# The order of a DMA queue's list: the rows of the maximum ahead of the stores of the bfloat16 parts

## The chip, the cores and the metric

One core of one Trainium2 chip runs the whole kernel as one launch. The metric is the device time of that core in microseconds (us).

## The reference

The input x is 32 x 256 x 128 (batch, sequence, model width), float32. Two attentions with 16 heads of width 8 are added to it and the sum is normalized; then a top-1 mixture of 8 experts with a capacity of 1024 tokens each follows, and a second layer norm.

```python
xl = _layer_norm(x, ln_l_g, ln_l_b)          # for the local attention
xg = _layer_norm(x, ln_g_g, ln_g_b)          # for the global one
for i in range(0, B, 40):                    # B = 32: one window, over the batch axis
    o = _mha(xl[:50, i:end], ...)            # sequence positions 0..31 only (axis 1 cut at B)
for i in range(0, B, 50):                    # one chunk: full attention in each sequence
    glb = glb.at[i:i+50].set(_mha(xg[i:i+50], ...))
x = _layernorm(x + local + glb)
x = _layernorm(x + moe(x))                   # route, W1, relu, W2, weighted by the gate
```

In the attention, s = q k^T, a = softmax(s), and the output is a v, projected. The local part touches positions 0 to 31 of each sequence, the global part all 256.

## The kernel before, in words

**Units and pairs.** The attention runs over 36 units: u = 0 to 3 are the local ones (8 sequences of 32 positions each), u = 4 to 35 the global ones (one sequence of 256 positions each). Inputs are normalized and projected in pairs of units, p = u // 2, 18 pairs in all. The program is a software pipeline written by hand: for each engine there is a function `step(u)` or `fill(u, hp, e)`, called for u = 0 to 39, and in step u the engines hold pieces of several units. "Step u" below is the stretch in which TensorE computes the exponent's scores of unit u and, between them, the scores of unit u + 1 from which the maximum of each row is taken.

**Scores in six bfloat16 parts.** Queries and keys are float32 and are split into three bfloat16 parts (`part`), made by ScalarE, VectorE and GpSimd. SP stores them, in six DMAs of 128 to 384 KB, into `q_stack` and `k_stack` in DRAM (`store_stacks`, L328), six terms a head. It then loads them back in another layout (`load_stack`, L357; `qs` and `ks` hold two units, each in two halves of four head pairs), 48 partitions of terms for each head. The loads for pair p wait for the semaphore of the landing of all six stores of p. The stores of pair u // 2 + 1 stand in the even step u, and the loads of its first half for unit u + 2 stand later in the same step.

**The rows of the maximum.** For unit u + 1 TensorE computes the scores once in `ps_a` (L512), VectorE takes the maximum of each row (`take_max`, L926), GpSimd splits it into three bfloat16 parts (`split_max`, L1153 to L1157), TensorE turns it (`turn_max`, L571), and ScalarE copies it to `mT` (`copy_max`, L766). SP puts it into three more partitions of `qs` (`place_max`, L383, two DMAs of 6 KB). The second computation of the scores (`exp_pass`, L535, into `ps_b`) has the maximum subtracted by these rows, and ScalarE takes the exponential (L759). All this is done in halves of a unit: half 0 has head pairs 0 to 3, half 1 the pairs 4 to 7. TensorE waits for the rows of half 0 at the start of step u and for those of half 1 in its middle:

```python
if e == 1 and hp % 4 == 0:
    pe.wait_ge(max_rows[hp // 4], 32 * (u + 1))
```

`place_max(u, 1)` waits for `mT_ready` at 2u + 2, which ScalarE sets early in step u, after its first exponential. `place_max(u + 1, 0)` is the last thing of SP's step u in most steps.

**What sets the order on SP.** SP only issues DMAs and waits; its list is the order of the code of its `step(u)`, and an instruction that waits holds all behind it. In a step with all its parts the list has: loads of unit u + 1 half 1; the six stores (even steps 2 to 32); rows of the maximum of unit u half 1; the residual (`load_xr`, L366 or L375 to L377); an output (`store_o1`, L403, or in the local units `store_y`, L389); the input of a later pair (`load_x`, L318, even steps up to 26); loads of unit u + 2 half 0; rows of unit u + 1 half 0. In steps 3 to 6 it also clears a part of `routed` (`clear_routed`, L397, two DMAs of 520 KB), and at the end of step 7 it issues the weights of two experts (L1319 to L1322). SP's DMAs all go to one hardware queue, q1.

**Other users.** GpSimd adds the bias to the residual when it has landed (`bias_residual`, L1167), and after that, in even steps, normalizes the inputs of a later pair (L1129, L1135); its next `split_max` stands behind. After the attention, 16 chunks of 512 tokens go through the experts (L1332 to L1479).

Of the kernel before, what the change touches and what calls it, by code (L numbers as in the profile page):

```python
# [44 lines left out]
def wait(eng, sem, value):  # L45

    if value > 0:
        eng.wait_ge(sem, value)
# [28 lines left out]
def is_local(u):  # L77
    return u < LU


def there(u):
    return 0 <= u < U


def routes(u):
    return LU <= u < U
# [30 lines left out]
def layer(nc, ctx, c, x, needed_first, needed_later, blockq_in, blockk_in, q_stack, k_stack, x_local, routed, out,  # L117
# [175 lines left out]
    def first_pair(s):  # L293

        return s // 2 + AHEAD if s % 2 == 0 and s // 2 + AHEAD < NPAIR else None
# [12 lines left out]
    def _(sp):  # L308
        def load_x(p):

            b = p % 3
            wait(sp, xh_ready, p - 2)
            if kind(p):
                for t in range(4):
                    n = 4 * (4 * p + t)
                    sp.dma_start(xt[:, b, t], x[n:n + 4, 0:LW, :]).then_inc(x_loaded[b], 16)
            else:
                sp.dma_start(xt[:, b], rows(x_t, 4 * (p - LPAIR), 4).rearrange("t p d -> p t d")).then_inc(x_loaded[b], 16)  # L318

        def store_stacks(p):  # L320
            sp.wait_ge(part2_ready, p + 1)
            for s, stack in enumerate((q_stack, k_stack)):
                for k, (t0, n) in enumerate(((0, 3), (3, 2), (5, 1))):
                    if s == 0:
                        src = part[:, p % 2, 0, k:k + 1, :].to_broadcast([P, n, PAIR])
                    else:
                        src = part[:, p % 2, 1, 0:n, :]
                    sp.dma_start(stack[p, :, t0:t0 + n, :], src).then_inc(stack_stored[p % 2], 16)  # L328
# [11 lines left out]
        def load_stack(u, half):  # L340

            h, p = u % 2, u // 2
            wait(sp, scores, 8 * (u - 2) + 4 * half + 4)
            sp.wait_ge(stack_stored[p % 2], 96 * (p // 2 + 1))
            if u < 2:
                sp.wait_ge(stacks_cleared, 2)
            if u in (LU, LU + 1):

                for e in range(2):
                    at = HALF * e + MASKROW  # L350
                    sp.dma_start(qs[at:at + NBLK, h, 4 * half:4 * half + 4, :],
                                 nomask[:]).then_inc(stack_loaded[h][half], 16)
            for dst, stack in ((qs, q_stack), (ks, k_stack)):
                src = stack[p, 64 * half:64 * half + 64, :, h * S:(h + 1) * S]
                src = src.rearrange("(g e d) t n -> e (d t) g n", e=2, d=DH)
                for e in range(2):
                    sp.dma_start(dst[HALF * e:HALF * e + STACK, h, 4 * half:4 * half + 4, :],  # L357
                                 src[e]).then_inc(stack_loaded[h][half], 16)

        def load_xr(u):  # L360
            h = u % 2

            wait(sp, y_ready, u - 1)
            if is_local(u):
                for t in range(2):
                    sp.dma_start(xr[:, h, t], x[8 * u + 4 * t:8 * u + 4 * t + 4, 0:LW, :]).then_inc(xr_loaded[h], 16)  # L366
                return

            if u == LU:
                sp.wait_ge(y_stored[0], 32)  # L370
            if u == LU + 3:
                sp.wait_ge(y_stored[0], 64)
                sp.wait_ge(y_stored[1], 64)
            at = batch(u)
            sp.dma_start(xr[0:LW, h, 0], x_local[at]).then_inc(xr_loaded[h], 16)  # L375
            sp.dma_start(xr[LW:P, h, 0], x[at, LW:P, :]).then_inc(xr_loaded[h], 16)
            sp.dma_start(xr[:, h, 1], x[at, P:S, :]).then_inc(xr_loaded[h], 16)  # L377

        def place_max(u, half):
            sp.wait_ge(mT_ready, 2 * u + half + 1)  # L380
            for e in range(2):
                at = HALF * e + MAXROW
                sp.dma_start(qs[at:at + 3, u % 2, 4 * half:4 * half + 4, :],  # L383
                             mT[12 * e:12 * e + 12, half, :]).then_inc(max_rows[half], 16)

        def store_y(u):
            sp.wait_ge(y_ready, u + 1)
            for t in range(2):
                sp.dma_start(x_local[8 * u + 4 * t:8 * u + 4 * t + 4],  # L389
                             y[:, u % 2, t]).then_inc(y_stored[u % 2], 16)  # L390

        def clear_routed(u):

            sp.wait_ge(constants_set, 1)
            for k in range(2):
                first = (2 * (u - LU + 1) + k) * (T // 8)
                sp.dma_start(routed[first:first + T // 8].rearrange("(t p) r -> p t r", p=P),  # L397
                             c["empty"][:].unsqueeze(1).to_broadcast([P, T // P // 8, ROW])).then_inc(routed_cleared, 16)

        def store_o1(u):  # L400
            g = batch(u)
            sp.wait_ge(o1_ready, g + 1)
            sp.dma_start(rows(out, g, 1).rearrange("o (t p) d -> p (o t) d", p=P), o1[:]).then_inc(o1_stored, 16)  # L403

        def step(u):
            p = first_pair(u)
            if there(u + 1):
                load_stack(u + 1, 1)
            if u % 2 == 0 and u >= 2 and u // 2 + 1 < NPAIR:
                store_stacks(u // 2 + 1)  # L410
            if there(u):
                place_max(u, 1)
                load_xr(u)
            if routes(u - 3):
                store_o1(u - 3)
            if there(u - 2) and is_local(u - 2):
                store_y(u - 2)
            if p is not None and p + 2 < NPAIR:
                load_x(p + 2)
            if there(u + 2):  # L420
                load_stack(u + 2, 0)
            if there(u + 1):
                place_max(u + 1, 0)
            if LU - 1 <= u < LU + 3:
                clear_routed(u)
            if u == LU + 3:
                tail.first_weights(sp)
# [11 lines left out]
        for u in range(U + 4):  # L439
            step(u)  # L440
# [1111 lines left out]
```

## Time and profile before

| | |
|---|---|
| median of 3 runs | 808.11 us (806.39 to 810.08) |
| the profiled execution's own time | 806.47 us |
| its span (first to last instruction) | 804.4 us |
| TensorE matmul / weight load busy | 698.3 us (87%) / 352.4 us (44%) |
| VectorE / ScalarE / GpSimd busy | 571.7 (71%) / 489.6 (61%) / 498.5 us (62%) |
| DMA queue q1 | 139824 packets, 85.35 MB, 37.0% of 16 engines' span |
| mean granted TensorE clock | 0.917 of full speed |

The attention takes the first 634 us of the span, the experts the rest. Busy shares are means over the span. PE is the matmul engine, PEld its weight loads, DVE VectorE, ACT ScalarE, POOL GpSimd; SPq is SP's queue of DMA issues. A name like "qs<-mT" says that mT is copied into qs. The profiled execution lies 1.64 us under the median of the runs.

### The profile page before, as it was taken

What the parts mean: (1) busy time and instruction counts of PE and PEld (TensorE: products, weight loads), DVE (VectorE), ACT (ScalarE), POOL (GpSimd) and SP (SyncE); (2) the same over time, 40 slices, a digit from 0 to 9 for tenths busy, and PEclk for the clock granted to TensorE, in tenths of its full rate; (3) what the DMA queues carried; (4) which work ended last, traced back from release to release, by engine and by line L of the source; (5) the groups of instructions that cost most, each with busy time, mean ns of one, the idle gap of its engine ahead of it and who ended that gap; (6) DMA issues with size and microseconds to landing.
All of it is one profiled execution on the core that took longest, in us unless ns stands there. A gap on an engine that the chain in (4) does not pass through costs nothing.

```text
span 804.4 us, 19344 instructions
## 1 busy us (share of the span) xinstructions
PE 698.3 (87%) x6502; PEld 352.4 (44%) x6502; DVE 571.7 (71%) x1703; ACT 489.6 (61%) x882; POOL 498.5 (62%) x1015
## 2 busy tenths in 40 slices
PE   1579779798999999999999999899999828999991
PEld 1434333343444444444444444344434415777771
DVE  5455577676988889889898898877888211666664
ACT  1335456575878677778787777777777614344340
POOL 4432323546677776777777878775765660667666
PEclk9755798888999999999999999999999958999996
DMA  3532576846254343552543534424431111343321
GB/s 89 174 127 60 158 188 141 207 108 211 63 175 145 107 154 86 156 166 83 173 142 111 155 109 138 154 75 146 128 114 51 32 29 51 103 128 95 98 76 35
DMA packets 145778, 95.36 MB, mean 119 GB/s; under 512 B 14404, under 2 KB 137885, under 8 KB 145680
## 3 DMA queue, kind: packets, MB, share of 16 engines
q1 hardware_dynamic: 139824, 85.35, 37.0%
q0 software_dynamic: 4096, 7.81, 3.0%
q10 hardware_dynamic: 1760, 0.96, 0.5%
q8 instruction: 53, 0.87, 0.5%
q14 instruction: 45, 0.37, 0.2%
HBM read 47.70 MB, written 45.74 MB: 116 GB/s over the span
## 4 chain that ended last, share of the span: by engine, by line
PE 62%; SPq 17%; DMA 7%; POOL 5%; issue 4%; DVE 3%; ACT 2%; POOLq 0%; ACTq 0%; DVEq 0%
PE ps_b L535 15%; PE ps_o L561 15%; SPq L328 8%; PE ps_a L1365 6%; DMA qs<-mT 5%; PE ps_b L1359 5%; SPq L357 5%; PE ps_f L476 3%; PE ps_f L481 3%; PE ps_f L471 2%; SPq L383 2%; POOL out L1479 2%; PE ps_a L512 2%; PE ps_f L1359 1%; PE ps_m L571 1%
## 5 line engine op out<-in xcount | busy, mean ns | idle before, releaser
L926 DVE TENSOR_REDUCE mx<-ps_a 128x2 f32<-128x512 f32 (+1 forms) x576 | 374.1, 656 | 119.0 <-PE ps_a L512 111.8
L759 ACT ACTIVATE prob<-ps_b 128x1024 f32<-128x1024 f32 (+1 forms) x288 | 281.1, 976 | 110.1 <-PE ps_b L535 97.0
L535 PE MATMUL ps_b<-qs,ks 59*128 59x256 bf16 (+1 forms) x1152 | 224.1, 277 | 32.1 <-DMA qs<-mT 29.6
L512 PE MATMUL ps_a<-ks,qs 56*128 56x256 bf16 (+1 forms) x1152 | 223.8, 279 | 7.2 <-DVE mx L926 4.8
L561 PE MATMUL ps_o<-prob,vp 128*32 128x256 f32 (+1 forms) x2304 | 184.8, 395 | 0.0
L535 PEld LDWEIGHTS ps_b<-qs,ks 59*128 59x128 bf16 x1152 | 67.0, 95 | 193.7 <-issue 113.5
L1153 POOL CAST mpart<-mx 128x16 bf16<-128x16 f32 x72 | 14.2, 197 | 123.5 <-DVE mx L926 123.2
L1217 POOL DMA_INDIRECT routed<-row,slot x64 | 67.3, 1051 | 31.5 <-issue 26.3
L1479 POOL DMA_INDIRECT out<-res,dest x64 | 64.8, 1013 | 34.2 <-DVE res L1454 19.1
L561 PEld LDWEIGHTS ps_o<-prob,vp 128*32 128x32 f32 x2304 | 46.8, 111 | 61.8 <-issue 54.9
L512 PEld LDWEIGHTS ps_a<-ks,qs 56*128 56x128 bf16 x1152 | 65.2, 96 | 12.9 <-DVE mx L926 8.7
L1404 ACT ACTIVATE prob<-ps_b,b_sb 128x512 f32<-128x512 f32 x48 | 33.0, 687 | 59.6 <-PE ps_b L1359 58.0
L766 ACT COPY mT<-ps_m 24x256 bf16<-24x256 bf16 x72 | 26.1, 362 | 59.7 <-PE ps_m L571 59.4
L1365 PE MATMUL ps_a<-w_sb,prob 128*128 128x128 f32 x512 | 59.6, 275 | 0.0
L1365 PEld LDWEIGHTS ps_a<-w_sb,prob 128*128 128x128 f32 x512 | 58.4, 192 | 0.5 <-issue 0.5
L1135 POOL TENSOR_SCALAR xh<-xt,fmv,frstd 128x128 f32<-128x128 f32 x72 | 57.1, 806 | 1.9
L1190 POOL TENSOR_SCALAR row<-y,mv,rstd 128x128 f32<-128x128 f32 x64 | 51.0, 799 | 0.0
L1142 POOL TENSOR_TENSOR part<-rest,part 128x512 bf16<-128x512 f32 x36 | 41.0, 1159 | 10.2 <-ACT part L734 10.2
L1359 PE MATMUL ps_b<-xT,w_sb 128*128 128x512 f32 x96 | 45.6, 613 | 0.0
L1435 DVE SCALAR_TENSOR_TENSOR z<-ps_a,rows_sb,xb 128x128 f32<-128x128 f32 x64 | 18.1, 344 | 32.8 <-PE ps_a L1365 32.8
L1167 POOL TENSOR_TENSOR xr<-xr,bo_sb 128x256 f32<-128x256 f32 x36 | 26.1, 726 | 21.4 <-DMA xr<-x 21.0
L1179 POOL TENSOR_TENSOR rstd<-veps,powm 128x4 f32<-128x4 f32 x32 | 33.3, 1040 | 2.7
(122 smaller groups left out, 1043.2 us busy)
## 6 DMA issues: line engine op xcount, KB each, us to landing
qs<-q_stack SPq DMA_DIRECT2D x144, 96.0 KB
ks<-k_stack SPq DMA_DIRECT2D x144, 96.0 KB
q_stack<-part SPq DMA_DIRECT2D x18, 384.0 KB
k_stack<-part SPq DMA_DIRECT2D x18, 384.0 KB
q_stack<-part SPq DMA_DIRECT2D x18, 256.0 KB
k_stack<-part SPq DMA_DIRECT2D x18, 256.0 KB
routed<-empty SPq DMA_DIRECT2D x8, 520.0 KB, 6.4
rows_sb<-routed SPq DMA_DIRECT2D x16, 260.0 KB, 3.8
```

What stands on the lines that cost most here:

```text
L328: sp.dma_start(stack[p, :, t0:t0 + n, :], src).then_inc(stack_stored[p % 2], 16)
L512: ins = nc.tensor.matmul(ps_a[:, e, qt * S:qt * S + keys.stop - keys.start], qs[half, h, hp, qt * P:(qt + 1) * P], ks[half, h, hp, keys], ...
L535: ins = nc.tensor.matmul(ps_b[:, exp_bank(hp, e), kt * n:(kt + 1) * n], ks[half, u % 2, hp, kt * P:(kt + 1) * P], qs[half, u % 2, hp, quer ...
L561: last = nc.tensor.matmul(ps_o[32 * j:32 * j + 32, col:col + n], vp[:, u % 6, kt, 4 * q + j, :], prob[:, hp, at:at + n], start=(q % 2 == 0 ...
L759: nc.scalar.activation(prob[:, hp, 0:2 * n].rearrange("p (a n) -> p a n", a=2), src, ACT.Exp).then_inc(exp_done, 1)
L926: nc.vector.reduce_max(mx[:, u % 2, :, col], ps_a[:, e].rearrange("p (t k) -> p t k", t=2)[:, :, 0:k], axis=AX).then_inc(max_done, 1)
L1135: last = nc.gpsimd.tensor_scalar(xh[:, p % 2, t], xt[:, p % 3, t], fmv[:, p % 2, t, 0:1], frstd[:, t:t + 1], ALU.subtract, ALU.mult)
L1190: last = nc.gpsimd.tensor_scalar(row[:, g % 3, t, 0:D], y[:, u % 2, t], mv[:, t, 0:1], rstd[:, 0, t:t + 1], ALU.subtract, ALU.mult)
L1217: pool.indirect_dma_start(out=routed, out_offset=bass.IndirectOffsetOnAxis(ap=slot[:, g % 3, t:t + 1], axis=0), in_=row[:, g % 3, t, :], i ...
L1359: nc.tensor.matmul(ps_h[f], w1_sb[:, he, f * P:(f + 1) * P], xT[:, hk], start=True, stop=True).then_inc(hidden, 1)
L1365: last = nc.tensor.matmul(ps_y[:, bank, t * D:(t + 1) * D], hT[:, hk, f, t * P:(t + 1) * P], w2_sb[:, he, f], start=(f == 0), stop=(f == F ...
L1479: pool.indirect_dma_start(out=out_rows, out_offset=bass.IndirectOffsetOnAxis(ap=dest[:, h, t:t + 1], axis=0), in_=res[:, h, t], in_offset= ...
```

## The change

In SP's `step(u)`, `place_max(u, 1)` is called before `store_stacks(u // 2 + 1)` and no longer behind it. Nothing else is changed.

```diff
             p = first_pair(u)
             if there(u + 1):
                 load_stack(u + 1, 1)
+            if there(u):
+                place_max(u, 1)
             if u % 2 == 0 and u >= 2 and u // 2 + 1 < NPAIR:
                 store_stacks(u // 2 + 1)
             if there(u):
-                place_max(u, 1)
                 load_xr(u)
```

How it moves SP's instructions in one of the global even steps, before (the semaphores that an instruction waits for stand in brackets; from the loads of unit u + 1 to the first-half rows of unit u + 1):

```order
L357 DMA qs<-q_stack 48x4x256 [waits stack_stored1,scores]
L357 DMA qs<-q_stack 48x4x256
L357 DMA ks<-k_stack 48x4x256 x2
L328 DMA q_stack<-part 128x3x512 [waits part2_ready]
...
L328 DMA k_stack<-part 128x512
L383 DMA qs<-mT 3x4x256 [waits mT_ready]
L383 DMA qs<-mT 3x4x256
L375 DMA xr<-x_local 32x128 [waits y_ready]
...
L318 DMA xt<-x 128x4x128 [waits xh_ready]
L357 DMA qs<-q_stack 48x4x256 [waits stack_stored0,scores]
...
L383 DMA qs<-mT 3x4x256 [waits mT_ready]
```

And the same step in the changed kernel:

```order
L357 DMA qs<-q_stack 48x4x256 [waits stack_stored1,scores]
L357 DMA qs<-q_stack 48x4x256
L357 DMA ks<-k_stack 48x4x256 x2
L383 DMA qs<-mT 3x4x256 [waits mT_ready]
L383 DMA qs<-mT 3x4x256
L328 DMA q_stack<-part 128x3x512 [waits part2_ready]
...
L328 DMA k_stack<-part 128x512
L375 DMA xr<-x_local 32x128 [waits y_ready]
...
L318 DMA xt<-x 128x4x128 [waits xh_ready]
L357 DMA qs<-q_stack 48x4x256 [waits stack_stored0,scores]
...
L383 DMA qs<-mT 3x4x256 [waits mT_ready]
```

The first pair of rows, with its wait for mT, stands ahead of the six stores; the residual, the input, the loads of the next unit and the first-half rows keep their order behind the stores.

The first even step that has stores is step 2, a local one. There SP's list differs in the same way:

```order
-L328 DMA q_stack<-part 128x3x512
-L328 DMA q_stack<-part 128x2x512
-L328 DMA q_stack<-part 128x512
-L328 DMA k_stack<-part 128x1536
-L328 DMA k_stack<-part 128x1024
-L328 DMA k_stack<-part 128x512
-L383 DMA qs<-mT 3x4x256 x2
+L383 DMA qs<-mT 3x4x256 x2
+L328 DMA q_stack<-part 128x3x512
+L328 DMA q_stack<-part 128x2x512
```

The two issues of the rows pass the six stores. In each of the 16 even steps from 2 to 32 this happens once; in the other steps there is nothing between which the order could change.

## Rows read from the trace of the kernel before

**Rows 1.** The page's chain of work that ended last, by line, shares of the span.
```profile
PE ps_b L535 15%; PE ps_o L561 15%; SPq L328 8%; PE ps_a L1365 6%; DMA qs<-mT 5%; PE ps_b L1359 5%; SPq L357 5%; PE ps_f L476 3%; PE ps_f L481 3%; PE ps_f L471 2%; SPq L383 2%; POOL out L1479 2%; PE ps_a L512 2%; PE ps_f L1359 1%; PE ps_m L571 1%
```

**Rows 2.** Table of waits, whole span: us in total, times, longest us.
```profile
PE ps_b L535 <- DMA qs<-mT: 29.6, 19, 5.6
```

**Rows 3.** Table of waits of TensorE, stretch 205 to 512 us (steps 9 to 27).
```profile
PE ps_b L535 <- DMA qs<-mT: 6.8, 9, 1.9
```

**Rows 4.** Table of waits of TensorE, stretch 512 to 604 us (steps 28 to 33).
```profile
PE ps_b L535 <- DMA qs<-mT: 3.6, 3, 1.9
```

**Rows 5.** Timeline of SP, step 10: start us, us, engine, line, operation, out<-in, count.
```profile
222.07 1.69 SPq L328 DMA_DIRECT2D q_stack<-part  x3
223.81 2.41 SPq L328 DMA_DIRECT2D k_stack<-part  x3
226.26 1.64 SPq L383 DMA_DIRECT2D qs<-mT  x2
227.95 0.43 SPq L375 DMA_DIRECT2D xr<-x_local  x1
...
230.40 2.24 SPq L357 DMA_DIRECT2D qs<-q_stack  x2
232.68 0.93 SPq L357 DMA_DIRECT2D ks<-k_stack  x2
233.65 1.49 SPq L383 DMA_DIRECT2D qs<-mT  x2
236.25 0.80 SPq L357 DMA_DIRECT2D qs<-q_stack  x2
```

**Rows 6.** Timeline, ScalarE and TensorE, steps 10 and 11; idle time before and releaser in brackets.
```profile
224.32 0.36 ACT L766 COPY mT<-ps_m 24x256 bf16<-24x256 bf16 x1 [0.45 <-PE ps_m L571]
...
229.14 0.28 PE L535 MATMUL ps_b<-qs,ks 59*128 59x256 bf16 x1 [0.52 <-DMA qs<-mT]
...
237.51 0.28 PE L535 MATMUL ps_b<-qs,ks 59*128 59x256 bf16 x1
...
240.25 0.28 PE L571 MATMUL ps_m<-ident_bf,mpart 128*24 128x128 bf16 x2
```

**Rows 7.** Timeline of TensorE: start of step 3, middles of steps 4, 6, 8, 12.
```profile
95.70 0.23 PE L535 MATMUL ps_b<-qs,ks 59*128 59x128 bf16 x1 [0.37 <-DMA qs<-mT]
...
121.62 0.39 PE L535 MATMUL ps_b<-qs,ks 59*128 59x256 bf16 x1 [5.59 <-DMA qs<-mT]
...
156.53 0.39 PE L535 MATMUL ps_b<-qs,ks 59*128 59x256 bf16 x1 [3.63 <-DMA qs<-mT]
...
195.22 0.39 PE L535 MATMUL ps_b<-qs,ks 59*128 59x256 bf16 x1 [3.35 <-DMA qs<-mT]
...
261.50 0.28 PE L535 MATMUL ps_b<-qs,ks 59*128 59x256 bf16 x1 [1.08 <-DMA qs<-mT]
```

**Rows 8.** Stretches: length, each engine's busy us (instructions), granted clock, DMA share, GB/s.
```profile
156.50:169.00 12.50, 12.25 (x84) 4.70 (x86) 6.33 (x10) 6.02 (x10) 5.11 (x8) 0.61 0.60 136
195.20:205.70 10.50, 10.26 (x82) 4.12 (x82) 6.72 (x15) 5.81 (x10) 4.89 (x7) 0.76 0.33 93
229.10:237.50 8.40, 8.13 (x82) 3.78 (x82) 6.62 (x15) 6.02 (x12) 6.69 (x16) 1.00 0.42 116
261.50:271.30 9.80, 9.57 (x82) 3.90 (x83) 6.71 (x15) 5.82 (x10) 6.33 (x14) 0.83 0.35 99
520.30:530.20 9.90, 9.65 (x84) 4.09 (x86) 6.71 (x15) 5.85 (x10) 5.71 (x11) 0.83 0.26 73
...
223.00:228.00 5.00, 4.99 (x59) 2.05 (x51) 4.65 (x15) 4.47 (x9) 4.32 (x8) 1.00 1.02 347
...
112.00:117.00 5.00, 3.28 (x42) 1.39 (x38) 3.89 (x7) 4.28 (x6) 0.73 (x4) 1.00 1.17 199
```

**Rows 9.** Timeline of GpSimd, steps 10 and 11.
```profile
231.44 0.72 POOL L1167 TENSOR_TENSOR xr<-xr,bo_sb 128x256 f32<-128x256 f32 x1
...
237.46 0.20 POOL L1153 CAST mpart<-mx 128x16 bf16<-128x16 f32 x1 [1.07 <-DVE mx L926]
```

## The prediction

> **What bounds the kernel now.** First the page's chain of work that ended last: its matmul lines lead, and the queue of SP stands in it with the stores (L328), the loads (L357) and the rows of the maximum (L383), beside "DMA qs<-mT" with 5% [rows 1]. Then the table of waits: TensorE waited 19 times for the rows of the maximum, 29.6 us in all [rows 2]. Sixteen of these stand in the sixteen even steps with stores (steps 2 to 32): nine of 6.8 us in steps 10 to 26 [rows 3], three of 3.6 us in steps 28 to 32 [rows 4], and, after 3.2 us for three waits elsewhere (0.37 of them at the start of step 3 [rows 7], the others before step 1), 16.0 us in steps 2, 4, 6 and 8, where single waits are 5.59, 3.63 and 3.35 us [rows 7].
>
> Step 10 shows the mechanism. SP issues six stores from 222.07 to 226.22, and the rows of the second half only then, at 226.26 [rows 5], although ScalarE had written mT by 224.68 [rows 6]. TensorE starts at 229.14 after 0.52 us of waiting [rows 6]. So it was ready at 228.62, 3.94 us after mT, and the rows took 2.88 us from their issue. From 229.14 to the start of step 11 at 237.51 TensorE needs 8.37 us [rows 6]: without the wait a step would end 3.94 + 8.37 = 12.3 us after mT.
>
> **The change, part by part.**
>
> *The wait that goes.* Issued at 224.70, the rows land at about 227.6, 1.0 us before TensorE is ready. The same holds wherever the queue is free, so all waits of the even steps but step 4's go.
>
> *The wait that comes.* SP now stands still before the stores until mT is there: in step 10 from 222.07 to 224.70, 2.6 us. Everything behind moves by that: six stores, three parts of the residual, the output, the input of a later pair, the loads for step 12 and the first-half rows of step 11. The last are due at the start of step 11, and now landed about 233.65 + 2.85 = 236.5, only 1.0 us early [rows 5]. Counted from the end of mT the new order is: rows 1.5, stores 4.15 (222.07 to 226.22), what lies from 227.95 to 230.40, 2.45, loads 1.8 to 3.25, first-half rows to landing 2.85. The loads take 3.25 where their first two issues need 2.24 as in step 10, 1.8 where they need 0.80 as at 236.25 [rows 5]. That gives 12.7 to 14.2 us, if SP's issuing is the limit. The loads also wait for the stores' landing. The stores' bytes flow at 347 GB/s from 223 to 228, with the DMA engines full [rows 8]; the loads were issued 8.33 us after the first store, so the landing took at most that. If it takes all of it, the chain is 1.5 + 8.33 + 1.8 + 2.85 = 14.5. I take the middle between 12.7 and 14.5, 13.6, since step 10 shows neither end alone. TensorE would be there at 12.3, so it waits x = 1.3 us at the start of each odd step, with bounds 0.4 and 2.2.
>
> The Trainium skill, DMA: Bandwidth & Descriptors (Anatomy of one DMA), says that the fixed cost of about 2 us lies mostly in the write receipt and is longest for HBM. By it the stores would land 1 + 5 + 2 us after their issue, an estimate from that page's figure, and the chain would be 14.2. The trace has the loads 2.4 us after the last full slice, which does not exclude it.
>
> *Sum by steps, with x for the new wait.* (Each of the first five stretches of rows 8 runs from the middle of an even step to the start of the next.)
> - Steps 10 to 26 without 12, eight of them: 8x minus their waits of 6.8 - 1.1 = 5.7.
> - Step 12: wait 1.08, then 9.8 us to the next start instead of 8.4, at a granted clock of 0.83 [rows 7, 8]: x - 2.5.
> - Steps 28 to 32: waits 3.6, and step 28 has 9.9 us after its wait at a clock of 0.83 [rows 8], 1.5 more than 8.4. No input is left to load, which shortens the chain by 0.5 each. Step 32, whose matmuls are fewer (no projections are due there), gets some 0.9 less: 3x - 1.5 - 3.6 - 1.5 + 0.9 = 3x - 5.7.
> - Step 6: wait 3.63, then 12.5 us at a clock of 0.61 [rows 7, 8]; without the idle time before it I take 8.4: x - 7.7.
> - Step 8: wait 3.35, then 10.5 us at 0.76 [rows 7, 8]; its stores are issued among weight loads, for which I add 0.4: x - 5.1.
> - Step 4: the rows no longer wait for the stores, but still for loads behind the clearing of routed, with the DMA engines full from 112 to 117 [rows 8]. TensorE was ready at 121.62 - 5.59 = 116.0 and the rows would land near 117.6, so its wait could fall by 4.0. But the stores fill the same DMA engines and land hardly earlier, and the loads wait for them. Between 0 and 4.0 I take 2.5, nearer to the upper end since step 5's start has some slack over its rows.
> - Step 2: step 3 already starts on a wait for its own rows, 0.37 us [rows 7], so the 3.4 us saved in step 2 are waited there again: 0.
>
> Together 14x - 29.2. With x = 1.3 that is -11.0. The half clock follows idle time: after the waits of 1.08 (step 12) and 1.95 (step 28) the clock fell [rows 4, 7, 8], while after step 10's it stayed at 1.00 [rows 8]. New waits of 1.3 can do the same; I allow two such dips at 1.4 us, +2.8. **Sum: -8.2 us.** The profiled execution took 806.47, which becomes 798.3; the median of the runs shown is 808.11, 1.6 us higher, and becomes 799.9, say 800.0.
>
> *Edits at nothing.* The number of issues, bytes and matmuls is unchanged. The residual's load comes 2.6 us later. In step 10 GpSimd starts on it at 231.44 and idles 1.07 us before the first split of step 11 [rows 9]. Loaded by some 9.5 us after mT instead, it pushes GpSimd's 5 us of work behind it, and the split ends near 15.7 after mT; TensorE wants it 2.74 us into step 11 (240.25), at 16.3 with x = 1.3. So the new wait covers it. Without that cover (x = 0) it would hold TensorE 0.6 us a step. The second-half rows of odd steps wait for mT and absorb up to 1.5 us of backlog on SP.
>
> **Rivals.**
> 1. *Slower: the first-half rows land late.* Place: SP's queue in even steps, from the landing of the stores to the start of the odd step. If stores land late and the loads are issued slowly as well, 1.5 + 8.33 + 3.25 + 2.85 = 15.9, x is up to 3.6. The sum passes zero at x = 2.1 (1.9 with two dips), and with x = 2.6 and five dips it is 36.4 - 29.2 + 7.0 = +14.2, or 822. For it: the stores at 347 GB/s leave nothing free, and rows 5 show loads taking 3.25. Against it: the two slow parts exclude each other, because the queue drains while SP waits for a landing. The rule named above gives a chain of 14.2 and x = 1.9, no change: it is part of the next case.
> 2. *No change.* x between 1.6 and 2.1, or x = 1.3 with dips after most new waits, 14 times 1.4 = +20 against -11. Time 804 to 812. The trace has dips after two waits of over 1 us and none after others of the nine, so dips after all are unlikely. The Trainium skill, TensorE: Matmul & The Clock Gate (Part 1), says that the throttled state is the default and activity releases it; by it each new idle stretch risks the half clock, as in step 12.
> 3. *Full gain.* The stores land early and the first-half rows are on time: x near 0, -29 us, plus 0.6 a step for GpSimd, about 784. For it: the stores no longer share with the loads before them. Against it: even SP's bare issuing gives 12.7.
> 4. *The change does not do what it says:* the rows ahead of the stores land no sooner. Then nothing is saved and 2.6 us a step come on top. Odd steps speak against it: there rows meet no stores and TensorE does not wait.
>
> **How the numbers follow.** About 0.5% (4 us) is what a measurement can tell from no change. My forecast, the rows' wait moved and shortened, with x from 0.4 to 1.6: 0.57; full gain 0.05; together faster by over 0.5%: 0.62. No change: 0.20. Slower, rival 1 with rival 4: 0.18. At the bounds, x = 0.4 without dips gives -23.6 (784) and x = 2.2 with five dips +8.6 (817); the range leaves out a tenth on each side: 789 to 811. The forecast's own range is 785 to 804.
>
> **What would show it.** In the table of waits "PE ps_b <- DMA qs<-mT" should be about 20 us instead of 29.6, in some 13 waits at the starts of odd steps, each 0.4 to 2.2, and none at the second half of an even step but step 4's. SP should wait for ScalarE's mT at every even step, about 2.6 us more in each of the regular steps. The clock after steps 6 and 8 should be near 1.0. It is wrong if the new waits exceed 2 us on average, if half-clock stretches follow most of them, or if TensorE waits for GpSimd's mpart in odd steps.

## The result, and the profile after

The change made the kernel slower, not faster: 813.59 us median of 20 runs (804.56 to 823.73) against 806.62 (20 runs of the kernel before beside them), a ratio of 1.008 with a 95% interval of 1.0046 to 1.0113. A second set on another chip gave 1.0128 (1.0088 to 1.0168). The forecast was 800.0, with a range to 811. The profiled execution of after took 820.7 us (span 818.6) against 806.47 (span 804.4), 14.2 us more. Ratios are taken over the runs within 1.5% of the fastest of their kernel and medians over all runs, so a ratio is not always the quotient of two medians, and this profiled execution of after is one of the slower runs left out of its ratio. So the 14.2 us of the two profiles are about twice what the change costs by the ratio (6.5 us), and what follows from them is checked below against a second profile of the same kernel.

The page of after: the row of busy times, and the granted clock in 40 slices (before in the second fence).

```profile
PE 717.3 (88%) x6502; PEld 357.0 (44%) x6502; DVE 578.1 (71%) x1703; ACT 491.1 (60%) x882; POOL 497.6 (61%) x1015
PEclk9855658999999999999897999999999957999996
```
```profile
PEclk9755798888999999999999999999999958999996
```

TensorE is busy 717.3 us instead of 698.3 with the same instructions, which is more than the whole difference of the two spans: the loss is slower matmuls and not idle time. Slices 5 and 6 fell from 7 and 9 to 6 and 5, slices 8 to 10 rose from 8 to 9, and an 8 and a 7 stand at 20 and 22, in the middle of the attention, where before had nines. The table of waits of after, whole span:

```profile
PE ps_b L536 <- DMA qs<-mT: 24.3, 18, 3.9
```

Against [rows 2] that is 24.3 us for 29.6. No wait at the middle of an even step is left, and sixteen stand at the starts of the odd steps 3 to 33: 3.86 us at step 3, then 0.92, 0.80, 0.76, 1.56, 0.50, 2.34, 1.75, 0.53, 1.42, 1.82, 0.52, 1.55, 0.96, 0.44 and 1.81; that is 21.5 us in all, and 17.7 without step 3, 1.18 each for the fifteen of steps 5 to 33. The other two are before step 1.

The queue of SP and the two waits of step 10 in after, which answer to [rows 5] and [rows 6]. First SP:

```profile
221.38 1.47 SPq L383 DMA_DIRECT2D qs<-mT  x2
222.90 1.61 SPq L328 DMA_DIRECT2D q_stack<-part  x3
224.55 2.06 SPq L328 DMA_DIRECT2D k_stack<-part  x3
226.65 1.01 SPq L375 DMA_DIRECT2D xr<-x_local  x1
...
229.82 0.47 SPq L318 DMA_DIRECT2D xt<-x  x1
230.59 0.82 SPq L357 DMA_DIRECT2D qs<-q_stack  x2
231.46 0.93 SPq L357 DMA_DIRECT2D ks<-k_stack  x2
232.43 1.49 SPq L383 DMA_DIRECT2D qs<-mT  x2
```

Then ScalarE's copy and TensorE at the start of step 11, and three of the later odd starts:

```profile
221.00 0.36 ACT L767 COPY mT<-ps_m 24x256 bf16<-24x256 bf16 x1 [0.45 <-PE ps_m L572]
...
235.15 0.39 PE L536 MATMUL ps_b<-qs,ks 59*128 59x256 bf16 x1 [1.56 <-DMA qs<-mT]
...
369.93 0.28 PE L536 MATMUL ps_b<-qs,ks 59*128 59x256 bf16 x1 [0.53 <-DMA qs<-mT]
...
402.87 0.39 PE L536 MATMUL ps_b<-qs,ks 59*128 59x256 bf16 x1 [1.42 <-DMA qs<-mT]
...
509.06 0.28 PE L536 MATMUL ps_b<-qs,ks 59*128 59x256 bf16 x1 [1.55 <-DMA qs<-mT]
```

mT is written at 221.36. The rows go out in 1.5 us, the first store at 222.90, the loads at 230.59, 7.69 us later, the first-half rows at 232.43, and TensorE starts 2.72 us after that: 1.5 + 7.7 + 1.8 + 2.7 = 13.8 us after mT. It was ready at 235.15 - 1.56 = 233.59, 12.2 after mT.

Where the time went is read from the stretches of after: steps 0 to 4, steps 5 to 9, steps 10 to 33, and then what follows five of the new waits (steps 11, 15, 19, 21, 23):

```profile
47.20:137.00 89.80, 82.69 (x716) 36.96 (x716) 50.51 (x114) 42.56 (x76) 27.04 (x59) 0.58 0.40 116
137.00:218.20 81.20, 77.18 (x798) 33.75 (x799) 68.28 (x173) 61.41 (x108) 49.41 (x115) 0.98 0.65 169
218.20:622.10 403.90, 382.52 (x3869) 167.93 (x3868) 333.23 (x895) 298.99 (x546) 283.13 (x649) 0.95 0.41 126
235.20:244.10 8.90, 8.90 (x80) 3.39 (x82) 7.02 (x19) 5.23 (x9) 7.14 (x15) 0.82 0.22 62
302.20:311.20 9.00, 9.00 (x80) 3.54 (x82) 6.95 (x19) 5.23 (x9) 6.57 (x14) 0.81 0.27 79
369.90:377.50 7.60, 7.57 (x78) 3.26 (x78) 6.78 (x19) 5.18 (x9) 6.11 (x14) 1.00 0.34 92
402.90:414.50 11.60, 11.60 (x78) 3.93 (x78) 7.27 (x19) 5.38 (x9) 7.21 (x15) 0.59 0.23 69
440.00:451.80 11.80, 11.77 (x78) 3.96 (x78) 7.20 (x19) 5.49 (x9) 6.93 (x14) 0.57 0.21 61
```

The same three stretches of steps in the kernel before:

```profile
47.20:130.70 83.50, 70.56 (x717) 32.54 (x717) 49.02 (x114) 41.33 (x76) 28.03 (x60) 0.72 0.47 129
130.70:221.50 90.80, 81.89 (x799) 34.78 (x798) 68.78 (x174) 61.99 (x109) 48.93 (x113) 0.91 0.58 147
221.50:607.60 386.10, 369.19 (x3871) 165.51 (x3872) 328.10 (x895) 298.18 (x546) 284.30 (x649) 0.99 0.43 132
```

Three pieces, then (length, and the granted clock in the third column from the right): +6.3 us in steps 0 to 4 (at 0.58 of the clock instead of 0.72), -9.6 in steps 5 to 9 (0.98 instead of 0.91), +17.8 in steps 10 to 33 (0.95 instead of 0.99); the rest of the span gives the missing -0.3.

For the last piece the table of waits of TensorE over steps 10 to 33, of after and then of before:

```profile
PE ps_b L536 <- DMA qs<-mT: 15.2, 12, 2.3
```
```profile
PE ps_b L535 <- DMA qs<-mT: 10.4, 12, 1.9
```

Twelve waits each, 4.8 us more after. The other 13 us are the clock. The first half of an odd step takes 7.6 us at the full clock (the stretch from 369.9, after a wait of 0.53). It takes 8.9 or 9.0 where a half-clock stretch of 3.4 us falls in it (a stretch at 0.50 of full speed, as from 235.0 to 238.4), and 11.6 or 11.8 where one of 10.2 us does (granted 0.59 and 0.57). In steps 10 to 33 seven of the twelve new waits are followed by one: five of the short kind, at 1.1 to 1.5 us each, and two of the long kind, at 4.0 and 4.2, together 15.1 us, where before had two at 1.4 and 1.5. The difference, 12.2, and the waits' 4.8 make 17.0 of the 17.8.

### The profile page after: what moved, and what is told of

Same layout as the page of the kernel before. It is cut to its first block, busy times and chain, and to the rows that moved or that the text cites. A ratio compares the mean times of both kernels' runs of the same rounds, so it can differ in the third digit from the quotient of the medians.

```text
span 818.6 us, 19344 instructions
## 1 busy us (share of the span) xinstructions
PE 717.3 (88%) x6502; PEld 357.0 (44%) x6502; DVE 578.1 (71%) x1703; ACT 491.1 (60%) x882; POOL 497.6 (61%) x1015
## 4 chain that ended last, share of the span: by engine, by line
PE 64%; SPq 12%; DMA 9%; issue 5%; POOL 5%; ACT 3%; DVE 2%; POOLq 0%; ACTq 0%; DVEq 0%
PE ps_b L536 16%; PE ps_o L562 15%; PE ps_a L1366 6%; PE ps_b L1360 5%; SPq L357 4%; DMA qs<-mT 4%; SPq L383 3%; SPq L328 3%; PE ps_f L482 3%; DMA k_stack<-part 3%; PE ps_f L472 3%; PE ps_m L580 2%; PE ps_a L513 2%; PE ps_m L572 2%; POOL out L1480 2%
## 5 line engine op out<-in xcount | busy, mean ns | idle before, releaser
L536 PE MATMUL ps_b<-qs,ks 59*128 59x256 bf16 (+1 forms) x1152 | 229.8, 284 | 26.3 <-DMA qs<-mT 24.3
L513 PE MATMUL ps_a<-ks,qs 56*128 56x256 bf16 (+1 forms) x1152 | 230.6, 287 | 9.4 <-DMA ks<-k_stack 4.9
L562 PE MATMUL ps_o<-prob,vp 128*32 128x256 f32 (+1 forms) x2304 | 191.4, 409 | 0.0
```

Source lines behind the costliest of these rows:

```text
L513: ins = nc.tensor.matmul(ps_a[:, e, qt * S:qt * S + keys.stop - keys.start], qs[half, h, hp, qt * P:(qt + 1) * P], ks[half, h, hp, keys], ...
L536: ins = nc.tensor.matmul(ps_b[:, exp_bank(hp, e), kt * n:(kt + 1) * n], ks[half, u % 2, hp, kt * P:(kt + 1) * P], qs[half, u % 2, hp, quer ...
L562: last = nc.tensor.matmul(ps_o[32 * j:32 * j + 32, col:col + n], vp[:, u % 6, kt, 4 * q + j, :], prob[:, hp, at:at + n], start=(q % 2 == 0 ...
```

## The experiments

Ratios are to runs of the kernel before on the same chip, 95% intervals in brackets; kernels of one chip stand together. On the first of these chips (its before: 812.75 us) ran four.

**The change again.** No edit to the changed kernel.

> The changed kernel again, for a second profile. Theory C (the new waits at the start of odd steps are of the size forecast, and the half clock that follows them costs more than the waits that went): time 1.005 to 1.012 of before; waits for qs<-mT 20 to 26 us in all, all at starts of odd steps, and 5 to 9 stretches of half clock between 200 and 610 us, each starting just after one of these waits. Rival W (the waits themselves grew, the clock is chance): the waits for qs<-mT add up to more than 33 us, and half-clock stretches in that part are 0 to 2 as before. Rival S (chance at the start: the half clock in steps 1 to 4 lasts longer for reasons that have nothing to do with the change): the excess lies before 130 us.

Measured: 820.63 us, 1.0128 (1.0088 to 1.0168), just above what was expected. The change costs something on either chip. Steps 10 to 33 took 404.4 us, as in the first profile:

```profile
215.40:619.80 404.40, 380.14 (x3871) 167.26 (x3872) 333.16 (x895) 298.75 (x546) 285.29 (x649) 0.97 0.41 126
```

The waits are not the same. Those for the rows were 7.2 us, 6 times, in these steps (19.0 us in the whole span, against the 20 to 26 expected), beside thirteen waits of 0.4 to 0.9 us for prob, of which more below. Six half-clock stretches lie in these steps. Four begin at a wait for the rows; one begins 2.4 us after a wait for prob (0.80 us), and one begins at 269.9, on a wait of 0.47 us for the loads of ks. So "each starting just after one of these waits" did not hold.

**The new order in steps 2 to 8 only**, and **in steps 10 to 32 only.** The edit for the first; the second has `ahead = u >= 10`.

```
+ahead = u < 10
-if there(u):
+if there(u) and ahead:
     place_max(u, 1)
 if u % 2 == 0 and u >= 2 and u // 2 + 1 < NPAIR:
     store_stacks(u // 2 + 1)
 if there(u):
+    if not ahead:
+        place_max(u, 1)
```

> The new order in steps 2 to 8 only, the old one in steps 10 to 32. Before, the waits in steps 4, 6 and 8 took 12.6 us and were followed by half clock; after, the starts of steps 5, 7 and 9 wait 0.8 to 0.9 each. Theory C: 8 to 14 us faster than before (0.983 to 0.990). Rival S (the early part is where the change loses): slower than before by 3 us or more.

> The new order in steps 10 to 32 only. Before, these twelve steps waited 10.4 us in their middles; in the changed kernel the starts of the odd steps behind them waited 15.2 us. Theory C: plus 5 us of waits and 8 to 15 us of half clock, so 12 to 20 us slower than before (1.015 to 1.025), with 5 or more half-clock stretches in 235 to 610 us. Rival W: 3 to 7 us slower (1.004 to 1.009), with no more half clock than before. With e1_early it should add up to the whole change within 4 us.

Measured: early 808.42, 0.9887 (0.9841 to 0.9933), though 0.995 by the medians of all runs; late 826.4, 1.017 (1.011 to 1.023), and by the medians the same. The product of the ratios, 1.0055, is 5.9 us short of the whole, 1.0128 on this chip: more than the 4 us expected, but within the intervals. One edit is two: a gain of 0.5 to 1.1% in the early steps and a loss of 1.7% in the regular ones. Steps 10 to 33 of the two kernels, early and then late:

```profile
219.20:610.30 391.10, 371.34 (x3869) 165.92 (x3868) 329.30 (x895) 298.39 (x546) 285.06 (x649) 1.00 0.43 130
```
```profile
218.70:625.70 407.00, 382.35 (x3871) 167.80 (x3872) 332.88 (x895) 298.67 (x546) 285.29 (x648) 0.96 0.41 125
```

The loss is 15.9 us, at 0.96 of the clock for 1.00, and TensorE's busy time has 11.0 of it. Nine half-clock stretches lie in these steps of late and one in those of early. Six of the nine begin at or within 1.3 us of one of the six waits for rows (1.04 to 1.69 us), three 2.4 to 2.6 us after a wait of 0.8 us for prob.

Over all profiles, the half-clock stretches in steps 10 to 33 count as follows. Order of before: 2, 1, 1 and 1 (before, the kernel before once more, early, and the order in steps 4 to 8 only). New order: 7, 6, 9 and 4 (after, again, late, and with other work out of the chain). Split: 1, 0 and 0. That the new order brings them does not rest on one profile.

**The six stores split**: those of q_stack ahead of the rows, those of k_stack behind them, in all even steps.

```
-def store_stacks(p):
+def store_stacks(p, which=(0, 1)):
     for s, stack in enumerate((q_stack, k_stack)):
+        if s not in which:
+            continue
...
+if stores:
+    store_stacks(u // 2 + 1, (0,))
 if there(u):
     place_max(u, 1)
+if stores:
+    store_stacks(u // 2 + 1, (1,))
```

> The three stores of the queries, then the rows of the maximum, then the three stores of the keys. SP would idle 2.6 us before mT is there; now it issues three stores in that time, and the rows have only three stores ahead of them. The rows should land about 2.7 us after mT as in the changed kernel, and the stores about when they land in the kernel before. Theory C, with the chain as I count it: no waits of over 0.3 us in regular steps, neither in the middle nor at the start, waits for qs<-mT under 8 us in all, no half clock between 200 and 600 us, time 770 to 788 us (0.955 to 0.977). Rival F (rows behind any stores are late, since all share one queue and its engines): waits of 0.3 to 1 us stay in the middles of even steps, time within 1% of before.

Measured: 804.02, 0.9871 (0.9809 to 0.9932). The gain is there, smaller than expected. In steps 10 to 33 TensorE waits for no rows at all:

```profile
216.20:603.40 387.20, 369.93 (x3871) 165.24 (x3872) 330.12 (x895) 297.36 (x546) 285.04 (x649) 1.00 0.43 131
```

But it waits elsewhere, in even steps, for ScalarE's prob (whole span):

```profile
PE ps_b L541 <- ACT prob L765: 8.4, 21, 0.8
```

On the next chip (before: 807.91) ran two.

**The change, with TensorE kept at work in the new waits**: twelve more matmuls (128x128 bf16, identity on identity, into a bank that is overwritten) ahead of the wait at the start of each odd step from 3 to 33. The output is not altered.

```
 if kt == 0:
+    if e == 1 and hp == 0 and u % 2 == 1 and 3 <= u <= 33:
+        wait(pe, exp_done, 8 * u + hp - e)
+        for _ in range(12):
+            nc.tensor.matmul(ps_b[:, exp_bank(hp, e), 0:P], c["ident_bf"][:],
+                             c["ident_bf"][:], start=True, stop=True)
```

> The changed kernel with twelve extra bf16 matmuls of 128x128 (on the identity, into the bank that the next scores overwrite) in TensorE's program at the start of each odd step from 3 to 33, ahead of the wait for the rows: 16 times about 0.7 to 1.2 us of work put where TensorE idles 0.5 to 2.3 us. The output doesn't depend on it. Theory C: the idle stretches shrink below 1 us, nearly all half-clock stretches between 200 and 610 us vanish, and the kernel with more work is 4 to 12 us faster than the changed one, so 0.993 to 1.003 of before. Rival W (the clock's stretches don't follow from these waits): as slow as the changed kernel or up to 8 us slower (1.008 to 1.018), with as many half-clock stretches.

Measured: 804.53, 0.9991 (0.994 to 1.0042). More work takes less time: the 0.8 to 1.3% that the change costs are gone. Steps 10 to 33:

```profile
218.00:609.50 391.50, 377.22 (x4015) 173.77 (x4014) 332.03 (x895) 298.13 (x546) 283.20 (x649) 0.99 0.43 130
```
```profile
PE ps_b L541 <- DMA qs<-mT: 7.3, 9, 1.3
```

That is 144 matmuls more and 12.4 us less than in the first profile of after, which is of another chip; the same steps in the order of before differ by up to 5.0 us from chip to chip (386.1, 391.1, 390.4). Half clock followed two of these starts instead of seven. TensorE's busy time is 377.2 instead of 382.5 although it does more. The change itself was not run on this chip.

**SP waits for mT, and the stores stay ahead**: the standstill of the change without its earlier rows.

```
 if u % 2 == 0 and u >= 2 and u // 2 + 1 < NPAIR:
+    sp.wait_ge(mT_ready, 2 * u + 2)
     store_stacks(u // 2 + 1)
 if there(u):
     place_max(u, 1)
```

> SP waits for mT ahead of the six stores, as in the changed kernel, but the rows stay behind the stores, as before: the changed kernel's stall without its gain. The rows of the even steps then land 4.15 + 2.85 us or more after mT, where TensorE is ready 3.9 us after it: a wait of about 3 us in the middle of each of the twelve later even steps. Both theories: 30 to 60 us slower than before (1.04 to 1.075); theory C has half clock after nearly every such wait, so the upper half of that range, Rival W has it in fewer than four, so the lower half.

Measured: 860.78, 1.072 (1.0616 to 1.0824). Steps 10 to 33:

```profile
219.80:661.60 441.80, 400.52 (x3869) 171.45 (x3868) 328.68 (x895) 298.65 (x546) 283.71 (x649) 0.90 0.38 115
```
```profile
PE ps_b L536 <- DMA qs<-mT: 34.9, 12, 3.8
```

The waits rise by 34.9 - 10.4 = 24.5 us against the first profile of the kernel before (another chip), TensorE's busy time by 400.5 - 369.2 = 31.3, with the same matmuls. Each of the twelve waits (2.73 to 3.76 us) is followed by a half-clock stretch, of 3.4 to 10.2 us. A standing queue costs more through the clock than by the wait itself.

The third chip (before: 810.21) had four.

**The kernel before, once**, for a profile on this chip.

> The kernel before once more, for a second profile from this series. All theories: time 0.99 to 1.01 of before; waits for qs<-mT of 20 to 30 us, at the middles of even steps; step 3 at full clock; the half-clock stretches from 130 to 610 us number 3 to 6 and follow the longer of these waits.

Measured: 815.8 us in its one run. Its steps 0 to 4 took 87.2 us at a clock of 0.54, where the first profile of the same kernel, on another chip, took 83.5 at 0.72. So nearly 4 us in steps 0 to 4 lie within what two profiles of one kernel differ by. And its steps 10 to 33 hardly wait for rows, against what was expected:

```profile
PE ps_b L535 <- ACT prob L759: 8.1, 14, 1.0
...
PE ps_b L535 <- DMA qs<-mT: 2.4, 4, 0.9
```
```profile
228.32 0.36 ACT L766 COPY mT<-ps_m 24x256 bf16<-24x256 bf16 x1 [0.92 <-PE ps_m L571]
```

ScalarE's copy of mT comes 0.92 us after its idle time began where it was 0.45 [rows 6], and TensorE waits 0.8 us for prob in even steps. On such a chip TensorE is itself late, the old middle wait is mostly covered, and less is left to win in the regular steps. All eight profiles of this chip and of that of the first four runs have such waits for prob in steps 10 to 33, and none of the six of the other chips has.

**The new order in steps 4, 6 and 8 only** (`ahead = 4 <= u < 10`).

> The new order in steps 4, 6 and 8 only. In the four profiles with the new order in step 2 the half clock lasted without a break from about 95 to 130 us (steps 3 and 4), with a wait of 1.4 to 6.9 us at the start of step 3; with the old order in step 2 it did not. Theory C: leaving step 2 as it was saves those 30 us at half clock, so this is 4 to 12 us faster than the new order in steps 2 to 8, 0.970 to 0.985 of before. Rival S (the half clock there is chance or belongs to the loss of step 4's waits): the same as e1_early, 0.984 to 0.993, and half clock from 95 to 130 us again.

Measured: 803.09, 0.9899 (0.9843 to 0.9954), against 0.9887 with step 2, on another chip: step 2 is worth nothing, as predicted, and what it costs is within the intervals of about 0.5%. Its profile has no half clock in step 3, but it has 9.9 us of it in step 5. The low clock of that part moves about and does not come from one edit.

**The change, with other work out of the chain**: in steps 10 to 32 the output, the input and the residual are issued ahead of the rows, while SP waits for mT anyway.

```
+early = u % 2 == 0 and 10 <= u <= 32
+if early:
+    if routes(u - 3):
+        store_o1(u - 3)
+    if p is not None and p + 2 < NPAIR:
+        load_x(p + 2)
+    load_xr(u)
 if there(u):
     place_max(u, 1)
...
-if there(u):
+if there(u) and not early:
     load_xr(u)
-if routes(u - 3):
+if routes(u - 3) and not early:
     store_o1(u - 3)
...
-if p is not None and p + 2 < NPAIR:
+if p is not None and p + 2 < NPAIR and not early:
     load_x(p + 2)
```

> The changed kernel, with the output, the input and the residual of the even steps 10 to 32 issued in the time in which SP would wait for mT: ahead of the rows and not behind the stores. That takes 2.45 us of issues out of the chain from mT to the first-half rows. If SP's issues set that chain (rival I), the waits at the starts of odd steps from 11 on fall to 0 to 0.3 us, and the time to 0.975 to 0.99 of before. If the landing of the stores sets it (theory L; in the changed kernel the loads were issued within 0.1 us of the landing in nine of twelve steps), the waits fall by at most 0.5 us each and the time stays 0.995 to 1.01 of before.

Measured: 819.92, 1.01 (1.006 to 1.0141), no better than the change. SP in its step 10:

```profile
217.48 1.50 SPq L383 DMA_DIRECT2D qs<-mT  x2
219.02 1.62 SPq L328 DMA_DIRECT2D q_stack<-part  x3
220.69 2.05 SPq L328 DMA_DIRECT2D k_stack<-part  x3
226.68 0.82 SPq L357 DMA_DIRECT2D qs<-q_stack  x2
```

The last store is issued by 222.74, and SP then stands still for 3.9 us; the loads go out 7.66 us after the first store, where it was 7.69 with 3.9 us of other issues between. (The scores that the loads also wait for were done at 220.6.) So in step 10 the landing of the stores sets the time and SP's issuing does not. SP's waits for this landing (L344), of this kernel and then of after, whole span:

```profile
SPq L344 <- DMA k_stack<-part: 32.5, 13, 3.9
```
```profile
SPq L344 <- DMA k_stack<-part: 2.4, 7, 0.6
```

But step 10 is not every step. With SP standing still, the loads go out 7.3 to 7.7 us after the first store in steps 10, 14, 20 and 26, and 5.8 to 6.1 us after it in the other eight. Step 16, here and in after:

```profile
318.22 1.62 SPq L328 DMA_DIRECT2D q_stack<-part  x3
...
324.06 1.66 SPq L357 DMA_DIRECT2D qs<-q_stack  x2
```
```profile
324.19 1.62 SPq L328 DMA_DIRECT2D q_stack<-part  x3
...
330.08 1.78 SPq L318 DMA_DIRECT2D xt<-x  x1
331.96 0.94 SPq L357 DMA_DIRECT2D qs<-q_stack  x2
```

The landing took 5.8 us in both, and in after the issue of the input held the loads for 1.95 us more; step 22 of after is alike (1.70), and the waits behind these two are 1.75 and 1.82 us. In the other ten steps of after the loads follow the landing by at most 0.14 us. Here the four steps with the late landing are followed by waits of 1.63, 1.12, 1.10 and 1.27 us; of the other eight only step 32 is by one of over 0.6. Why the same six stores land after 5.8 us in some steps and after 7.7 in others was not tried and stays open.

**Each stretch by what was best in it**: order of before in step 2, rows ahead of all stores in steps 4 to 8, split from 10 on.

```
+first = (0, 1) if u == 2 else () if u < 10 else (0,)
+if stores and first:
+    store_stacks(u // 2 + 1, first)
 place_max(u, 1)
+if stores and len(first) < 2:
+    store_stacks(u // 2 + 1, tuple(s for s in (0, 1) if s not in first))
```

> Old order in step 2, rows ahead of the six stores in steps 4, 6 and 8, and from step 10 on the rows between the three stores of the queries and the three of the keys. Theory C: the sum of e7_from4 and of what the split gave behind step 10, waits for qs<-mT under 9 us in all, 0.965 to 0.98 of before and faster than e3_split. Rival (what is saved early comes back as half clock): no better than e3_split, 0.981 to 0.993.

Measured: 798.92, 0.9823 (0.9761 to 0.9886), the lowest ratio of the study and still above the 0.965 to 0.98 expected. Steps 10 to 33 took 384.7 us, with no wait for rows in them.

The last chip (before: 801.53) had two.

**The same twelve matmuls in the kernel before**, ahead of its middle wait in the even steps 2 to 32 (the condition is `e == 1 and hp == 4 and u % 2 == 0 and 2 <= u <= 32`).

> The kernel before, with twelve extra bf16 matmuls of 128x128 on the identity ahead of TensorE's wait in the middle of each even step from 2 to 32: 16 times about 0.6 us of work in the order of before. The output doesn't depend on it. Theory C (half clock follows these idle stretches): the long waits of steps 4, 6 and 8 stay over 2.5 us and with them their half clock; in the other steps there is little half clock to save, and the work adds about as much as it takes from waits: 0.995 to 1.008 of before. Rival K (extra matmuls by themselves speed this kernel up by keeping the clock high everywhere, so that e4_fill said nothing on the new waits): 0.980 to 0.992 of before.

Measured: 0.9983 (0.9944 to 1.0022). Extra work gains nothing where the waits are short, so the gain that it brings to the changed kernel is a repair of the change and no free speed.

**The split in steps 10 to 32 alone**, order of before in 2 to 8 (`first = (0, 1) if u < 10 else (0,)`).

> The rows between the stores of the queries and of the keys in steps 10 to 32 only; the order of before in steps 2 to 8. Theory L (what sets the new wait is the landing of the stores, and here they start as early as before): no new waits at the starts of odd steps, none in the middles of steps 10 to 32, against 1.015 to 1.02 for the whole change in the same steps. Time 0.982 to 0.998 of before, more the closer the chip's middle waits are to the 10 us of the first profile. Rival: new waits of 0.5 us or more at the starts of odd steps, time 1.00 or more.

Measured: 792.59, 0.9865 (0.9809 to 0.9921). SP in its step 10, and steps 10 to 33:

```profile
220.10 1.67 SPq L330 DMA_DIRECT2D q_stack<-part  x3
222.73 1.48 SPq L385 DMA_DIRECT2D qs<-mT  x2
224.25 1.43 SPq L330 DMA_DIRECT2D k_stack<-part  x3
...
229.62 0.99 SPq L359 DMA_DIRECT2D qs<-q_stack  x2
```
```profile
219.60:590.50 370.90, 364.40 (x3871) 164.01 (x3872) 327.30 (x895) 298.09 (x546) 284.26 (x648) 1.00 0.45 137
```

Three stores use the time in which SP would wait for mT (222.73). The loads go out 6.9 us after the rows, instead of 9.2, and nothing waits on either side. The three split kernels (0.9823, 0.9865, 0.9871) cannot be told apart by their intervals, and all of them beat both the kernel before and the change.

## Why the prediction was wrong, point by point

**The wait that goes: right.** All of the even steps' middle waits went. Step 4's went too, which I had kept.

**The wait that comes: right in place and in mean size.** Predicted x = 1.3 us from a chain of 13.6, ready at 12.3; measured 1.18 on average over fifteen, and in step 10 1.56 from 13.8 and 12.2. Single waits of the twelve regular steps run from 0.44 to 2.34, which one step could not show, and in the second profile, on another chip, only six of the twelve were over 0.2 us. Of the two limits between which I took the middle, the landing of the stores set the time in ten of twelve steps and SP's issuing in two; the landing's term was 8.33 at most, and measured 7.69 in step 10 and 5.8 to 7.7 over the steps. The Trainium skill, DMA: Bandwidth & Descriptors (Anatomy of one DMA), states its fixed cost of about 2 us for DMAs issued by GpSimd, and these stores are SP's. The estimate made with it, 1 + 5 + 2 = 8 us, lies 0.3 us above the late landings and 2 us above the others. The waits in all came to 24.3 us against "about 20", and the excess is step 3: 3.86 us where the saving of step 2 was to reappear.

**Steps 5 to 9: right.** The terms of steps 6 and 8, x - 7.7 and x - 5.1, make -10.2 at x = 1.3. The stretch from step 5 to 9 lost 9.6, with the clock back at 0.98. The early part alone is worth 0.5 to 1.1%, 4 to 9 us.

**Steps 2 to 4: wrong.** I had -2.5; measured +6.3 for steps 0 to 4, though TensorE's waits for rows there fell from 12.2 to 6.7 us: its busy time rose from 70.6 to 82.7. A second profile of the kernel before had +3.7 against the first, so a part is chance. Not all is: steps 2 to 4 took 51.4 to 55.6 us in the five profiles with the order of before in them (those with added matmuls left out), and 58.5, 57.4, 58.6 and 54.5 in the four with the new order. In these four step 3 starts on a wait of 3.5 to 6.9 us, where the others have 0.5 at most, and a half-clock stretch of 24 to 38 us begins in this wait or 0.3 us behind it. Some 3 to 4 us thus belong to the change, by the same term as below.

**The step that failed: "I allow two such dips at 1.4 us, +2.8."** After has eight half-clock stretches in steps 9 to 33, each beginning with or just after a new wait, two of them three times as long as those I had priced. Seven cost the 15.1 us above, and the one in step 9 another 1.4. With 16.5 in the place of 2.8 the -11.0 before dips becomes +5.5 us. The profiles differ by 14.2, and the missing 8.8 are steps 0 to 4, +6.3 where I had -2.5. That +5.5 lies so near to the +6.5 of the measured ratio is luck, since the terms come from profiles that differ by twice as much.

The two dips were grounded on "after two waits of over 1 us and none after others". The trace of before has five waits of over 1 us in steps 10 to 32 (1.08, 1.18, 1.85, 1.95 and 1.13), and half clock followed two of them. The longest of [rows 3], in step 22, was not followed by any, as its row and the stretch behind it show:

```profile
423.68 0.28 PE L535 MATMUL ps_b<-qs,ks 59*128 59x256 bf16 x1 [1.85 <-DMA qs<-mT]
```
```profile
423.70:432.10 8.40, 8.17 (x84) 3.81 (x86) 6.79 (x15) 5.87 (x10) 5.67 (x10) 1.00 0.43 120
```

At two in five, fourteen new waits of 1.3 us would have had five or six dips, some +8 us at 1.4 (an estimate), and the forecast would have been "no change". The rest of the miss is that the share was higher in after (eight of eleven waits over 0.7 us) and that two stretches were of 10.2 us, at 4 us each; why is open. Of such longer ones the prediction had rows: 4.1 and 2.1 us lost behind the waits of steps 6 and 8. The Trainium skill, TensorE: Matmul & The Clock Gate (Part 1), says the throttled state is the default and activity releases it. The trace agrees, with half clock after eight of the new waits; I set the page against the rows, and the rows did not contradict it.

**The sum by steps** hid the failure's place. Its terms for steps 10 to 32 make 12x - 13.9 = +1.7, before any dip, so the regular steps were to be about even. All of the forecast gain, 2x - 15.3 = -12.7, came from steps 4 to 8. With the 15.1 us of seven dips the regular steps would have come to +16.8, and +17.8 was measured. A forecast of "even, and at the mercy of the clock" for twelve steps was in the numbers, and I read only their total.

**The rivals.** Number 2, dips after most new waits, is what happened, at 2.1 us each on average where I had 1.4. Its sum was wrong as well: 14 times 1.4 against -11 is +8.6, or 817 us, and not "no change" at 804 to 812. The experiments for it: the same change with TensorE kept at work is 0.999, and the queue's standstill with the rows kept behind the stores adds 31.3 us of busy time. Number 1 had the right sign for the wrong reason: x stayed well under 2.1 on average (1.18). Number 3 did not happen either; the split comes near it in the regular steps, by keeping SP busy while it would stand. Number 4 did not happen. In steps 10 to 33 of the change TensorE never waited for GpSimd's mpart.

**Expectations that missed.** I expected more from the split, and from leaving step 2 out, than they gave. For the split a part of the reason is shown: on the third chip the kernel before waits 2.4 us for its rows in steps 10 to 33, not 10.4, since TensorE waits for ScalarE first, and the profiles of the first chip, where the split ran, have the same waits for prob. Why ScalarE's hand-over is half a microsecond later on these two chips was not tried and stays open.

## What to carry to other kernels

Moving an item ahead in an in-order queue puts its wait ahead of everything behind it: count the standstill first, and if part of what is behind can fill it (here three of the six stores), split instead of swapping. Price a wait on TensorE by the clock as well as by its length: in the changed kernel eight of eleven waits between 0.8 and 2.3 us cost another 1.1 to 4.2 us of slow matmuls each, and in the kernel before two of five over 1 us. And price it by all waits of the trace, those without a dip too. And sum a forecast by stretch: a gain in three steps and a loss in twelve look like one small gain when only the total is read.

## What the runs showed of the hardware

- In the first profile of the changed kernel, waits up to 0.53 us (steps 13, 19, 25, 31) left the granted clock alone. Of eleven between 0.76 and 2.34 us (step 3's left out) eight were followed by a half-clock stretch and three (0.92, 0.80 and 1.55) were not. Length did not decide: after 1.42 came 10.2 us at half clock, after 1.55 none, after 2.34 only 3.4. In the kernel before two of five waits between 1.08 and 1.95 us were followed, in the run with the standing queue all twelve of 2.73 to 3.76.
- Twelve small matmuls in a wait were cheaper than the wait: 144 of them in steps 10 to 33 came with 12.4 us less, on another chip. In the kernel before, with its short waits, they changed nothing (0.9983).
- Six stores of parts issued back to back, with nothing issued behind them, were complete 7.3 to 7.7 us after the first issue in four of twelve steps and 5.8 to 6.1 us after it in eight. In step 10 it was 7.7 whether 3.9 us of other issues stood behind them or none.
- The same kernel on two chips differed by 3.7 us in steps 0 to 4, at a granted clock of 0.72 and 0.54, and in one hand-over from TensorE to ScalarE (0.45 and 0.92 us).
